# A fused GNN, scan and LSTM kernel: the residual add behind the B product, the centring product half a slot later, a store on ScalarE's queue

## What is computed

```python
h = relu(adj @ layernorm(x) @ gcn_w + gcn_b)          # adjacency product: the bulk of TensorE's work
h = layernorm(h) * ln_g + ln_b
xz = h @ w_in; xc, z = split(xz)                      # Mamba block, D_INNER 256, D_STATE 16
u = silu(causal_conv4(xc) + conv_b)
dbc = u @ w_xp; dt = softplus(dbc[:, :8] @ w_dt + b_dt); B, C = rest of dbc
state = exp(dt * A) * state + dt * B * u              # a scan over 8192 tokens, 16 states for each of 256 channels
y = ((state @ C) + u * D_skip) * silu(z)
x1 = x + y @ w_out                                    # the residual
x = x1 + lstm_part(layernorm(x1))                     # an LSTM over 8192 tokens, then prefix and suffix sums
```

## Time and profile before

| | us |
|---|---|
| median of 3 runs (range) | 1605.08 (1603.58 to 1605.31) |
| the profiled execution's own time | 1600.95 |
| its span | 1598.9 |
| steps 3 to 15, from 206 to 1186 us of the span | about 75.2 each |
| drain, steps 16 to 18 | 1186 to about 1346 |
| LSTM and sums | from about 1346 |

### The profile page before, as it was taken

One profiled execution on the slowest core, in us unless ns is written; L12 is line 12 of the kernel. 1 busy time (PEld: TensorE's weight loads), 2 busy tenths in 40 slices (PEclk: granted clock), 3 DMA queues, 4 the chain that ended last, 5 costly groups with the idle time before them and its releaser, 6 DMA issues. The chain is left out here.

```text
span 1598.9 us, 17964 instructions
## 1 busy us (share of the span) xinstructions
PE 1511.9 (95%) x5006; PEld 772.3 (48%) x5006; DVE 1369.9 (86%) x1623; ACT 1040.0 (65%) x2210; POOL 1123.2 (70%) x536
## 2 busy tenths in 40 slices
PE   8999999999999999999999999999987688999994
PEld 3444444444444444444444444444432235998993
DVE  7406999999999999999999999999988695667998
ACT  3254766667676767675767666676768666777772
POOL 0325989898989898898989898989898761001221
PEclk9999999999999999999999999999989899999997
DMA  9877767677776776777777777776720203000002
GB/s 368 332 251 260 263 225 250 241 254 248 248 262 232 254 246 239 236 253 262 244 254 246 252 249 248 258 243 239 254 97 9 99 1 119 0 0 1 0 0 105
DMA packets 60491, 313.51 MB, mean 196 GB/s; under 512 B 6492, under 2 KB 6544, under 8 KB 27525
## 3 DMA queue, kind: packets, MB, share of 16 engines
q1 hardware_dynamic: 49537, 293.30, 52.8%
q10 hardware_dynamic: 10884, 19.41, 3.8%
HBM read 300.36 MB, written 12.32 MB: 196 GB/s over the span
## 5 line engine op out<-in xcount | busy, mean ns | idle before, releaser
L586 PE MATMUL bank<-ring,xh 128*128 128x512 f32 x2048 | 956.3, 594 | 13.2 <-DVE xh L1179 7.9
L1295 DVE TENSOR_TENSOR_SCAN work<-bank,hstate,work 128x512 f32<-128x512 f32 x512 | 628.1, 1268 | 29.9 <-ACT bank L881 24.4
L586 PEld LDWEIGHTS bank<-ring,xh 128*128 128x128 f32 x2048 | 387.9, 190 | 464.6 <-issue 422.6
L1065 POOL TENSOR_TENSOR work<-work 128x1024 f32<-128x1024 f32 x210 | 495.5, 2359 | 85.6 <-DVE work L1244 77.2
L881 ACT ACTIVATE bank<-work,a_neg 128x512 f32<-128x512 f32 x512 | 344.3, 686 | 226.1 <-DVE work L1295 225.4
L1236 DVE TENSOR_TENSOR work<-work,bank 128x1024 f32<-128x1024 f32 x256 | 310.1, 1217 | 62.0 <-POOL work L1041 50.8
L1244 DVE TENSOR_TENSOR work<-work,bank 128x1024 f32<-128x1024 f32 x168 | 201.2, 1198 | 20.8 <-POOL work L1065 20.8
L480 PE MATMUL bank<-bc_parts,sel 96*128 96x512 bf16 x456 | 172.0, 386 | 28.1 <-DVE work L1236 12.8
L475 PE MATMUL bank<-work,w_sb 128*128 128x512 f32 (+2 forms) x352 | 178.1, 602 | 5.9 <-ACT work L795 2.7
L1140 POOL TENSOR_TENSOR work<-work 128x256 f32 x32 | 28.6, 894 | 215.5 <-ACT work L944 215.5
L1010 POOL TENSOR_TENSOR work<-work 128x1024 f32<-128x1024 f32 x48 | 113.5, 2365 | 18.9 <-ACT work L755 18.7
(11 more groups left out here) (153 smaller groups left out, 1595.4 us busy)
## 6 DMA issues: line engine op xcount, KB each, us to landing
ring<-adj_t SPq DMA_DIRECT2D x256, 1024.0 KB, 5.6
work<-c_scratch ACTq DMA_DIRECT2D x28, 256.0 KB, 5.5
c_two<-c_scratch ACTq DMA_DIRECT2D x28, 256.0 KB, 5.1
xh<-x_rows SPq DMA_DIRECT2D x16, 256.0 KB, 7.0
work<-x_t SPq DMA_DIRECT2D x16, 256.0 KB, 5.4
x_scratch<-work ACTq DMA_DIRECT2D x16, 256.0 KB, 3.8
work<-x_scratch SPq DMA_DIRECT2D x1, 4096.0 KB, 14.1
out_t<-work SPq DMA_DIRECT2D x16, 256.0 KB, 2.4
```

The costliest lines, as they stand in the source:

```text
L586: last = nc.tensor.matmul(mixed[:, :], xn[:, j, :], a, start=(j == 0), stop=(j == BLK - 1))
L1065: nc.gpsimd.tensor_tensor(out=acc, in0=hc[0] if n == 1 else acc, in1=hc[n % 2], op=ALU.add).then_inc(y_added, 1)
L1295: nc.vector.tensor_tensor_scan(hb[s % 2][:, h, :], da[h], dbu[s % 2][:, h, :], hstate[:, HV * s + h:HV * s + h + 1], ALU.mult, ALU.add).th ...
```

## The change

Three edits. VectorE's residual add leaves `side_part` and comes behind `make_dbu(s+1)` of the same slot, ahead of the scans. `pcen` moves from 12.5 to 13, so from the middle of slot 12 to the start of slot 13 (in the drain from the middle of slot 13 to the start of slot 14, there behind that slot's `spread_b` and `spread_c`). The store of `xlc` in steps 4 to 15 leaves SyncE's queue and is issued by ScalarE in slot 5, behind `save_state`.

```diff
-          ("out", 11.5, "post"), ("pcen", 12.5, "post"), ("pvar", 13.5, "post")]
+          ("out", 11.5, "post"), ("pcen", 13, "post"), ("pvar", 13.5, "post")]
...
                         r = j % RING
-                        if j == 6 and not (isinstance(k, int) and k < 4):
-                            sp.wait_ge(xl_ready, k - 3)
-                            sp.dma_start(xl_dram[k - 4, 1:P, :], xlc[1:P, :]).then_inc(xl_stored, 16)
                         wait(sp, adj_used, PIECES * k + (j - RING + 1))
...
                         post_deviation(k - 1, True, True, (1,))
+                    if s == 5 and 4 <= k < NC:
+                        act.wait_ge(xl_ready, k - 3)
+                        act.dma_start(xl_dram[k - 4, 1:P, :], xlc[1:P, :]).then_inc(xl_stored, 16)
                     if scan and not drains(k) and s in C_LOAD:
                         load_c(C_LOAD[s])
...
                 def side_part(slot):
-                    s, t = planned(k, slot, "pre"), planned(k, slot, "post")
+                    s = planned(k, slot, "pre")
...
-                    if post and t == 12:
+                    if pre and s == 3:
+                        dve.wait_ge(rstd_ready, k)
+                        nc.vector.tensor_tensor(out=ht, in0=ht, in1=shared[:, :], op=ALU.mult).then_inc(shared_read, 1)
+                def add_x1(slot):
+
+                    if post and planned(k, slot, "post") == 12:
                         written("out")
                         dve.wait_ge(xt_in[q], 8 * (k - 3 - q) + 16)
                         wait(dve, x1_stored, 16 * (k - 3))
                         nc.vector.tensor_tensor(out=x1c, in0=xt[q], in1=shared[:, :], op=ALU.add).then_inc(shared_read, 1)
-                    if pre and s == 3:
-                        dve.wait_ge(rstd_ready, k)
-                        nc.vector.tensor_tensor(out=ht, in0=ht, in1=shared[:, :], op=ALU.mult).then_inc(shared_read, 1)
...
                     if not scan:
+                        add_x1(s)
                         continue
...
                     if s < DS - 1:
                         make_dbu(s + 1)
+                    add_x1(s)
                     for h in range(HV):
```

## The result

After the change the kernel takes 1661.91 us (median of 4 runs, 1659.96 to 1665.41), before it 1604.76 on the same chip (4 runs, 1603.58 to 1605.31). The ratio is 1.0367, with a 95% interval of 1.0354 to 1.038: 57 us slower. The forecast was 1692, the range 1640 to 1716. The sign is right and the time in the range, but 30 us of the forecast loss did not come. The profiled execution is the longest of the four (1665.41, span 1663.5), so against before (span 1598.9) it has 64.6 us to explain.

What follows compares the result with a forecast made beforehand. Bound: a loop of VectorE (50.1 us) and GpSimd (25.1), 75.2 a step. 1600.95 + 83 (late C row) + 4 (drain) = 1688 for the profiled execution; 1605.1 + 87 = 1692 for the median; range 1640 to 1716.

Steps and rivals of the forecast that it cites:

- The loop as the bound: Steps 3 to 15: VectorE's 50.1 us and GpSimd's 25.1 form a loop that sets the 75.2 us period.
- 0.8 of room: TensorE is nearly full but waits 0.8 us a step for VectorE, so it follows with little room.
- The residual add at 0: Slot 12: VectorE waits for the B row instead of the output product; change 0, also in steps 16 to 18.
- rival four: VectorE's 13.4 us of waits for the output product are gained, less the drain's 4: 1596, faster; chance 0.06.
- The centring product: Change 0 in steps 3 to 15; drain +2.6 us or up to 4 in step 16, +0.8 in step 18, taken as 4.
- The one engine: The store's 127 rows all go through a single DMA engine at 25 GB/s, holding it for 10.4 us.
- The late C row: C row 8, behind the store in ScalarE's queue, lands about 1012.6, delaying GpSimd's hc(8): 6.9 us a step, 12 steps, 83 us.
- rival two: The store gets more of the engine than a load did, 16 lines a turn or half the time: 1620 to 1660; chance 0.12.
- the cost of the issue: On ScalarE, issuing the store takes some 0.33 us, with 2 us of slack before the next exp is used: 0.
- TensorE's clock: Weighed in the drain only: if the clock returns later in step 16, the 2.6 us there become up to 4.
- The wait before L1086: Sign of being right: GpSimd idle some 7 us on the C row in slot 9, released by a DMA, 12 times.
- the 17 that was named as a sign of being wrong: The C row landing in under 17 us would show the forecast wrong; some 24 us would show it right.

Runs made afterwards that it cites:

- Relieving TensorE alone: Kernel before with its store on SyncE cut into 112 and 15 rows, so piece 6 lands sooner: 1603.89 against 1602.81, ratio 1.0003.
- the early load: Changed kernel with the load of C row 8 issued in slot 4 instead of 6, ahead of the uncut store: 1606.16 against 1602.81, ratio 1.002.
- slot 10: Changed kernel with the uncut store issued by ScalarE in slot 10 instead of slot 5: 1606.42 against 1603.6, ratio 1.0015.
- the last two above: Kernel before with dt·u product behind add(13) and SyncE's store cut in two: 1589.62; the same plus residual add behind the B product: 1586.86.

## Why the prediction was right, and where it was wrong

**The loop as the bound: confirmed.** The forecast's first reading, 50.1 us of VectorE and 25.1 of GpSimd closed in a ring, held from both sides. Relieving TensorE alone changed nothing (1.0003), and taking 2.37 us out of GpSimd's run gave 12 us, until TensorE became the bound after 0.7 us a step, where the forecast had given it 0.8 of room.

**The residual add at 0: right.** Alone it measures 0.9992 with 1.0 within the interval just barely, and rival four, a gain of 9 us and more, falls with it. Its ground was the right one: GpSimd's run decides when hc(15) starts, not VectorE's arrival.

**The centring product: right in steps 3 to 15 (period 75.32 against 75.29), about the size forecast in the drain.** Five kernels hold this edit and no trouble in the queue: alone, with either cut of the store, with the early load and with slot 10. They measure 1.0015 to 1.0022, which is 2.1 to 3.4 us, against 4 forecast; the intervals of three of them take in 4. Their profiles show 4.1 to 6.1 more in the drain stretch. Single profiles of this stretch differ by 2 us without a known reason, so whether 4 was too dear isn't settled. The place was right: the scan at the end of step 16 came 2.7 later, with 2.6 forecast.

**The one engine: right.** Cutting 127 rows into 112 and 15 ends every part of the loss. The rule of the Trainium skill cited ahead (DMA: Bandwidth & Descriptors, Why a DMA increments its semaphore by 16 and not by 1), that 127 partitions go to a single engine, agrees with that too.

**The late C row: the mechanism right, the term too large.** "6.9 us a step" measured 5.3 in step 7, the cleanest step of that form. Store and load were 3.9 us apart, not 3.0, and from the store's issue to the landing it was 26.5 us, where the forecast had 27.2. GpSimd came to the row 21.2 us after the store's issue, where the forecast took 20.2. These 0.7 and 1.0 are the difference of 1.6. (The 0.8 us that the sum took from the last line to the semaphore measures 0.3 to 0.5 in the loads of row 8 before the change.) So the sharing of the engine, one line of the store to one packet of a piece, fits a store as well; rival two, with more lines a turn, would have given 21.6 to 24.6. The rule of the Trainium skill weighed there (DMA: Bandwidth & Descriptors, Queues, rings and completion order: whole packets of typically 9 to 17 descriptors) is that rival, and 26.5 us doesn't agree with it.

**The step that failed is the cost of the issue:** "the issue, some 0.33 us beside work of its pipeline, and 2 us of slack before the next exp is used: 0". This held for the store's own issue (0.24 us) and was taken to hold for the next one on that queue. In ten of twelve steps the load's issue behind the store took 1.6 to 6.0 us, and ScalarE, which has compute work behind it in program order, stood for as long. In eight of these steps that is a stall of TensorE and in the end of VectorE. It isn't a loss on top of the 6.9, it takes its place: a step that lost its 5 us ahead of the row has the row in time. The row itself then comes sooner too, in step 13 18.6 us after the store's issue and not 26.5; SyncE issues no piece there between 1034.4 and 1044.4, as TensorE stands, so the one engine has less to share. That is why the total is 57 and not 87: 5.0 us a step from two forms of the same backlog, instead of 6.9 from one.

**A second term was put at nothing: TensorE's clock in steps 4 to 15.** The forecast weighed the clock for the drain alone. It made 1.8 of the 5.0 us a step.

**So the range was met in part by luck.** The path that was forecast, the late C row, holds up GpSimd in five of the twelve steps only, and is worth less there than forecast. What filled the gap, the stalled issue and the clock, wasn't in the sum. The direction, the edit at fault and the shape of the transfer as the cause were not luck: the runs with one edit each and with the cut store show them.

The kernel before showed the long issue already, in rows that I did not read for this. On SyncE, whose queue held the store then, the piece behind the store takes 3.1 to 3.7 us to issue in ten of the twelve steps (in step 5 it takes 0.71 and in step 13, the example step of the rows, 0.85). Here the piece of step 4, and the x_t load behind the lone store of step 16:

```profile
298.18 3.10 SPq L393 DMA_DIRECT2D ring<-adj_t  x1
```

```profile
1194.17 0.25 SPq L385 DMA_DIRECT2D xl_scratch<-work  x1
1194.46 3.39 SPq L382 DMA_DIRECT2D work<-x_t  x1
```

There nobody pays, since SyncE does nothing but issue and the store's cut on that queue gains nothing (1.0003). The same stall on ScalarE is paid by three engines.

**Signs named ahead.** The wait before L1086 came, 5 times and not 12; the landing took 22.6 us in step 7, not 24, but only 14.4 to 15.1 in six steps, under the 17 that was named as a sign of being wrong; periods were 80.3, not 82; pieces landed in 4.6 to 7.4 us in slots 5 to 9 of step 13; VectorE's wait moved to the B row.

## What to carry to other kernels

Before a DMA is moved to another engine's queue, list what is issued behind it there within its own duration, and what compute work that engine has behind those issues. A long issue cost nothing here on the engine that only issues, and was a stall on the one that computes. When a stall reaches TensorE, look at the granted clock behind it: here that was a third of the loss. The shape of the transfer comes first: 127 rows on one DMA engine, cut into 112 and 15, cost nothing that could be measured on either queue, and a wait is worth removing only on the loop that sets the period, which moving 2.4 us within GpSimd's program showed at once.

## What the runs showed of the hardware that was not expected

The issue of a DMA can take long when a transfer on one DMA engine is ahead of it in the same queue: 1.6 to 6.0 us instead of 0.33 on ScalarE, 3.1 to 3.7 on SyncE, in ten of twelve steps on either. How far the store had come is seen in the queues' packets, step 13, from 1030 to the end of the long issue at 1038.9 (q10 is ScalarE's), and then step 7 up to its load's issue, which was short:

```profile
q1 hardware_dynamic: 282, 2.06, 63.2%
q10 hardware_dynamic: 49, 0.10, 3.9%
```

```profile
q10 hardware_dynamic: 20, 0.04, 5.0%
```

In step 13 the issue ended when 49 of the store's 127 lines had gone, with 78 left; in six of the ten long ones it was 48 or 49, in the others 36, 45, 45 and 52. With the store cut in 61 and 66 rows no issue was long. That looks like a limit on what may be outstanding, but step 7 speaks against a simple one: with 20 lines gone, as few as in step 13 when its load was issued, its issue took 0.34 us. Steps 7 and 15, eight apart, are the two short ones. They are so again with the store alone moved (0.34 us both), and on SyncE in the kernel before the two short ones are steps 5 and 13, eight apart too. So it goes by the step and not by chance; what tells these steps from the others stays open. Open too is why the drain differs by 2 us between profiles of kernels that differ in it by the residual add alone (158.7 and 156.6 in the last two above), when that add alone left it at 158.8.
